# A graph layer pair on one core: VectorE scales the fourth of each four gathered chunks, GpSimd the other three

## The reference, cut to what matters

```python
    ex = jnp.exp(alpha - amax[dst])                             # one weight per edge and head
    denom = jax.ops.segment_sum(ex, dst, num_segments=n)
    attn = ex / jnp.maximum(denom[dst], 1e-10)
    out = jax.ops.segment_sum(h_src * attn[..., None], dst, num_segments=n)
    return out.reshape(n, H * D) + bias
x = _layernorm(x + _L1_gnn_ref(...), axis=-1)
```

## Time and profile before

| | |
|---|---|
| median of 3 runs | 3034.06 us (3033.27 to 3036.22) |
| the profiled execution, its own time | 3035.49 us |
| its span in the profile | 3033.7 us |
| granted TensorE clock, mean | 0.923 |
| busy over the span | PE 80%, DVE 56%, ACT 33%, POOL 62% |
| the weighted sum: from the first scale to the last add | 2730.5 to 2982.2 us |
| busy in 2780.77 to 2970.34 us (189.57 us, 320 adds, so 20 loop bodies) | PE 152.80, DVE 111.99, ACT 165.05, POOL 151.29 us |

### The profile page before, as it was taken

The page is one execution under the profiler, slowest core; times in us unless marked ns, Lnnn a source line. Parts: engine busy times, 40 slices in busy tenths (PEclk is TensorE's granted clock), DMA queues, the critical chain, the costliest instruction groups (busy, mean ns, idle before and its releaser), DMA issues.

```text
span 3033.7 us, 46185 instructions
## 1 busy us (share of the span) xinstructions
PE 2438.7 (80%) x9398; PEld 1579.2 (52%) x9399; DVE 1702.3 (56%) x4008; ACT 993.5 (33%) x2944; POOL 1880.7 (62%) x1739
## 2 busy tenths in 40 slices
PE   6999976477777679999899999999777767708882
PEld 5888843255555544445444454445555555506661
DVE  7765559899999940001344301113677666675557
ACT  1222221377777720000000000000433333318882
POOL 4777777787777870000067777760777777737774
PEclk9999999699999999999999999998888888859996
DMA  4000010355555555443344444452677777737772
GB/s 128 3 4 3 3 25 3 115 184 183 183 183 182 183 184 154 134 132 110 100 125 122 118 128 129 136 145 72 187 217 219 219 218 218 207 65 218 228 228 83
DMA packets 425353, 415.42 MB, mean 137 GB/s; under 512 B 85090, under 2 KB 411193, under 8 KB 424633
## 3 DMA queue, kind: packets, MB, share of 16 engines
q1 hardware_dynamic: 367385, 348.28, 36.8%
q0 software_dynamic: 57888, 66.23, 9.7%
HBM read 247.08 MB, written 167.17 MB: 137 GB/s over the span
## 4 chain that ended last, share of the span: by engine, by line
PE 54%; POOL 12%; issue 11%; DVE 7%; DVEq 4%; DMA 4%; ACT 3%; SPq 3%; ACTq 1%; POOLq 0%
PE psum L896 27%; POOL gath L618 7%; PE psum L826 5%; PE psum L708 5%; POOL rows_by_pair L579 5%; PE psum L693 3%; DVEq L400 2%; ACT lw L1084 2%; PE psum L888 2%; PE psum L968 2%; DMA gath<-gat_rows,rec 2%; SPq L484 2%; PE psum L1013 1%; PE psum L767 1%; PE psum L684 1%
## 5 line engine op out<-in xcount | busy, mean ns | idle before, releaser
L604 POOL DMA_INDIRECT rows_by_dst<-rec,place x392 | 381.6, 974 | 512.8 <-DVE place L1441 385.1
L896 PE MATMUL psum<-a_t,acc 128*128 128x512 f32 (+1 forms) x1400 | 553.7, 551 | 0.0
L589 POOL DMA_INDIRECT rows_by_low_digit<-rec,place x392 | 459.8, 1173 | 128.0 <-issue 128.0
L618 POOL DMA_INDIRECT gath<-gat_rows,rec x416 | 401.4, 965 | 214.1 <-issue 115.5
L826 PE MATMUL psum<-rhot,lw 128*128 128x256 f32 x1440 | 371.1, 414 | 169.7 <-ACT lw L1084 143.0
L579 POOL DMA_INDIRECT rows_by_pair<-rec,place x392 | 385.3, 983 | 161.9 <-issue 126.8
L826 PEld LDWEIGHTS psum<-rhot,lw 128*128 128x128 f32 x1440 | 281.9, 205 | 258.9 <-ACT lw L1084 182.2
L896 PEld LDWEIGHTS psum<-a_t,acc 128*128 128x128 f32 x1400 | 257.3, 195 | 272.1 <-issue 268.3
L1549 DVE SCALAR_TENSOR_TENSOR merged<-merged,same_of,psum 128x256 f32<-128x256 f32 x720 | 298.2, 476 | 19.1 <-PE psum L826 17.0
L896 PE MATMUL psum<-a_t,x 128*128 128x512 f32 (+1 forms) x700 | 294.4, 549 | 0.0
L1084 ACT ACTIVATE lw<-lhot,recs_pair 128x128 f32<-128x128 bf16 x720 | 228.5, 388 | 178.2 <-DVE lhot L1532 138.2
(11 more groups left out here) (311 smaller groups left out, 3301.9 us busy)
## 6 DMA issues: line engine op xcount, KB each, us to landing
a_t<-adjacency SPq DMA_DIRECT2D x450, 256.0 KB, 2.7
adjacency<-merged SPq DMA_DIRECT2D x721, 128.0 KB
gat_h_by_edge<-gath SPq DMA_DIRECT2D x104, 528.0 KB, 4.1
gath<-gat_h_by_edge SPq DMA_DIRECT2D x104, 528.0 KB, 4.1
gath<-gat_rows,rec POOLq DMA_INDIRECT x416
rows_by_pair<-rec,place POOLq DMA_INDIRECT x392
rows_by_low_digit<-rec,place POOLq DMA_INDIRECT x392
rows_by_dst<-rec,place POOLq DMA_INDIRECT x392
```

Source lines behind the costliest of these rows:

```text
L589: pool.indirect_dma_start(out=rows_low, in_=rec[:, c, :], out_offset=bass.IndirectOffsetOnAxis(ap=place[:, 1, c:c + 1], axis=0), in_offset ...
L604: pool.indirect_dma_start(out=rows_dst, in_=rec[:, c, :], out_offset=bass.IndirectOffsetOnAxis(ap=place[:, 0, c:c + 1], axis=0), in_offset ...
L618: pool.indirect_dma_start(out=gath[:, g % 4, c % 4, :], out_offset=None, in_=hh_dram, in_offset=bass.IndirectOffsetOnAxis(ap=rec_i[:, c, 0 ...
L896: i = pe.matmul(sums[b], table_g[:, w, b * P:(b + 1) * P], a_t[:, q % NA, 0:width(g)], start=False, stop=w == USED - 1)
```

## The change

VectorE gets a new instruction, `scale_fourth`: it scales the fourth chunk of a group, 128x256 elements, with both operands in SBUF. GpSimd's instruction is cut from four chunks to three. TensorE waits for the new semaphore `s_val4` before the fourth matmul of a group, and SyncE waits for it too before it refills a slot. The fourth chunks of groups 0 and 1 are scaled ahead of VectorE's wait for `s_clr`; the one of group g + 1 stands ahead of the adds of group g - 1, at even q ahead of the register load too. Four semaphores of earlier stages are folded into two others; each instruction still waits for the same event.

```diff
@@ -543,4 +543,5 @@
             for g in range(4, NQ):
                 sp.wait_ge(s_val, g - 3)
+                sp.wait_ge(s_val4, g - 3)
                 load_kept(g)
...
                     nc.gpsimd.tensor_tensor(
-                        val[:, q % 2, :, 0:D].rearrange("p c (h d) -> p c h d", h=HEADS),
-                        gath[:, q, :, 0:HX].rearrange("p c (h d) -> p c h d", d=HW)[:, :, :, 0:HD],
-                        s_sb[:, bass.ds(4 * g, 4), :].unsqueeze(3).broadcast_to([P, 4, HEADS, HD]),
+                        val[:, q % 2, 0:3, 0:D].rearrange("p c (h d) -> p c h d", h=HEADS),
+                        gath[:, q, 0:3, 0:HX].rearrange("p c (h d) -> p c h d", d=HW)[:, :, :, 0:HD],
+                        s_sb[:, bass.ds(4 * g, 3), :].unsqueeze(3).broadcast_to([P, 3, HEADS, HD]),
                         ALU.mult).then_inc(s_val, 1)
...
                     for j in range(4):
+                        if j == 3:
+                            pe.wait_ge(s_val4, g + 1)
                         if not (first and q < 2):
                             pe.wait_ge(s_add, 4 * (g - 2) + j + 1)
...
+            def scale_fourth(g, q, b, first):
+                dve.wait_ge(s_ld[q], 16 * (b + 1))
+                if not first:
+                    dve.wait_ge(s_mm, 4 * (g - 1))
+                v.tensor_tensor(val[:, q % 2, 3, 0:D].rearrange("p (h d) -> p h d", h=HEADS),
+                                gath[:, q, 3, 0:HX].rearrange("p (h d) -> p h d", d=HW)[:, :, 0:HD],
+                                s_sb[:, bass.ds(4 * g + 3, 1), :].rearrange("p c h -> p (c h)").unsqueeze(2)
+                                .broadcast_to([P, HEADS, HD]), ALU.mult).then_inc(s_val4, 1)
+
+            dve.wait_ge(s_exs, len(quads))
+            scale_fourth(0, 0, 0, True)
+            scale_fourth(1, 1, 0, True)
             dve.wait_ge(s_clr, 2)
 
             def sum_chunks(b, first, last):
                 for q in range(4):
                     g = 4 * b + q
+                    if not (first and q == 0) and not (last and q == 3):
+                        scale_fourth(g + 1, (q + 1) % 4, b + (q == 3), False)
                     if q % 2 == 0:
                         c = 1 + 4 * (g - 1)
...
-            act.wait_ge(s_seed, 1)
+            act.wait_ge(s_hist, 4)
...
-            dve.wait_ge(s_sum, 1)
+            dve.wait_ge(s_hist, 2)
...
-            dve.wait_ge(s_cum, 1)
+            dve.wait_ge(s_hist, 3)
...
-                dve.wait_ge(s_win, 1)
+                dve.wait_ge(s_ex, 2)
```

More of the change, by code:

```diff
@@ L271, in build @@
         s_oh = sem("onehots_built")
-        s_hist = sem("histogram_done")
+        s_hist = sem("histogram_product_done")
         s_part = sem("histogram_blocks_copied")
-        s_sum = sem("histogram_blocks_summed")
         s_hd = sem("histogram_step")
-        s_cum = sem("row_starts_summed")
-        s_seed = sem("table_seeded")
         s_hiT = sem("window_onehot_transposed")
@@ L302, in build @@
         s_place = sem("digit_places_ready")
-        s_ex = sem("window_starts_turned")
+        s_ex = sem("window_starts_turned_and_counted")
         s_exc = sem("window_starts_stored")
-        s_win = sem("windows_counted")
         s_low = sem("records_scattered_by_low_digit")
@@ L385, in build @@
         s_vx = sem("exp_columns_copied")
+        s_val4 = sem("fourth_chunk_scaled")
         s_mm = sem("chunk_summed")
@@ L671, in _ @@
             pe.wait_ge(s_part, 4)
-            pe.matmul(bank[1][0:HI, 0:LO], fold[:, :], blocks[:, :], start=True, stop=True).then_inc(s_sum, 1)
+            pe.matmul(bank[1][0:HI, 0:LO], fold[:, :], blocks[:, :], start=True, stop=True).then_inc(s_hist, 1)
             pe.wait_ge(s_hd, 6)
-            pe.matmul(bank[1][0:HI, 0:1], triu[0:HI, 0:HI], small[:, 0:1], start=True, stop=True).then_inc(s_cum, 1)
+            pe.matmul(bank[1][0:HI, 0:1], triu[0:HI, 0:HI], small[:, 0:1], start=True, stop=True).then_inc(s_hist, 1)
             pe.wait_ge(s_hd, 10)
             pe.matmul(bank[2][0:HI, 0:LO], identf[0:HI, 0:HI], table0[:, :], start=True, stop=False,
-                      skip_group_check=True).then_inc(s_seed, 1)
+                      skip_group_check=True).then_inc(s_hist, 1)
             def spread(t, s, n, cold):
@@ L757, in dst_windows @@
                 pe.wait_ge(s_exc, 2)
-                pe.matmul(bank[7][0:1, 0:NC], ones[0:USED, 0:1], started[0:USED, :], start=True, stop=True).then_inc(s_win, 1)
+                pe.matmul(bank[7][0:1, 0:NC], ones[0:USED, 0:1], started[0:USED, :], start=True, stop=True).then_inc(s_ex, 1)
                 yield
```

## The result

| | before | changed |
|---|---|---|
| median | 3035.14 us (3033.27 to 3036.54, 4 runs) | 3069.1 us (3067.64 to 3071.76, 4 runs) |
| ratio, 95% interval | | 1.0112 (1.0100 to 1.0124): slower |
| the profiled execution, its own time | 3035.49 us | 3068.21 us |
| its span | 3033.7 us | 3066.0 us |
| start of the first scale | 2730.52 us | 2731.55 us |

The forecast was 3066 us in a range of 3050 to 3088. The median is 34.0 us longer and the span of the profiled execution 32.3 us. Of that 31.2 us lie in the stage, 1.0 us ahead of it and nothing behind it. Of the change only the folded semaphores reach ahead of the stage.

A forecast was written before the change was run, and what follows sets the result against it. VectorE's own stream of adds and register loads was taken as the bound: 17.0 us at odd q, 12.3 at even q and 2.8 at the start make 32.1 us, so a median of 3066 us, range 3050 to 3088.

The forecast's parts named there:

- What bounds the stage: Stage 2730 to 2982 us: VectorE's adds and register loads are the bound, not GpSimd; four groups take 9.49 us.
- Odd q: Multiply between two groups' adds costs one datapath step, 0.34 us, 50 times: 17.0 us.
- second rival: VectorE's multiply slips into the adds' latency and costs nothing; only the start is left, 3037 us; chance 5%.
- Even q: Multiply ahead of the register load costs only sequencer steps, 0.18 us, or 0.31 at the loop's head: 12.3 us.
- The wait of the even multiply for the products: Ahead of the register load: products known at T + 2.65, margin 0.1 to 0.2 us, cost 0; otherwise 10 us.
- T: Time of VectorE's first add behind a register load (2853.88 us in the profile before).
- The collision: GpSimd's multiply holds VectorE's even multiply until T + 4.2; it ends at T + 4.5, hidden by the register load.
- third rival: The register load waits for a held multiply: 1.4 us in each of 50 pairs, 70 us more, 3136 us; chance 9%.
- GpSimd's time: GpSimd's instruction loses some 478 of 1913 ns, 104 times; it becomes idle time, value 0.
- The start: At the stage's start the first add of group 1 comes 2.8 us later, behind products and register load.
- The clock's case: Fourth rival: longer TensorE pauses lower its clock in the stage ten times, 15 us more, 3081 us; chance 14%.

The follow-up runs named there:

- e1: Kernel before, GpSimd scaling only three of four chunks, the fourth left as ones, nothing added to VectorE: ratio 0.9994, stage 251.0 us.
- e11: Kernel before with four slots of scaled rows in `val` instead of two: 3036.0 us against 3036.0, ratio 1.0000, stage 251.5 us.
- e3: Changed kernel with GpSimd's multiply cut to 8 columns of one chunk a group: ratio 1.0073 against the kernel before, stage 282.6 us.
- e7: Kernel before with four window numbers per register load instead of eight, each used twice: ratio 0.9962, stage 235.9 us.
- e5: Changed kernel with VectorE's multiply only between two groups' adds, GpSimd scaling four chunks of the other groups: ratio 1.0044, stage 270.0 us.
- e4: Changed kernel with VectorE's multiply only ahead of the register load, GpSimd scaling four chunks of the other groups: ratio 1.0045, stage 271.1 us.
- e2: Changed kernel with the even multiply moved behind the register load: ratio 1.0175 against the kernel before, stage 326.2 us.
- e9: Kernel before with window numbers packed in pairs (four loaded, taken apart in the sequencer), plus the change: ratio 0.9996, stage 253.9 us.
- e0: Changed kernel again, no edit, on other chips: 4293.0 us against 4260.1 for the kernel before, ratio 1.0084, stage 283.9 us.
- e6: Kernel before with the four folded semaphores alone: 4261.8 us against 4257.0, ratio 1.0010, stage 251.2 us.

## Why the prediction was right, point by point

- **What bounds the stage.** VectorE's own stream, and in it the register load, was the bound. e1 and e11 loosen GpSimd and change nothing, and so does e3 for the changed kernel; e7 shortens the load and gains the 16 us that it was expected to gain. This was the step on which everything hung, and it was read from the order in time against the name in the list of waits.
- **Odd q.** Forecast 0.34 us, measured 0.333, e5 alone 0.34. 50 x 0.333 = 16.7 us (17.0). The second rival, a free multiply, falls.
- **Even q.** Forecast 0.18 and 0.31 us, measured 0.23 and 0.32 us: 25 x 0.23 + 25 x 0.32 = 13.7 us (12.3).
- **The wait of the even multiply for the products.** At q = 2 of the body shown, ScalarE learns of the products at 2868.58, T + 2.65 as forecast, and VectorE's multiply begins at 2868.98, 3.05 behind its first add. The margin holds in the change. In e4, without the odd multiply ahead, it doesn't, and costs about 0.12 us each time: the condition that the prediction named.
- **The collision.** GpSimd's instruction was forecast at T + 2.8 and came at T + 2.79; its end, T + 4.2 forecast, was T + 4.27; the multiply's end T + 4.5 forecast, T + 4.55 measured; the second GpSimd instruction meets no multiply. The third rival (the load waits for the held multiply) falls by the chain above: the load starts 1.1 us ahead of the multiply's end. e3 shows that the hold costs nothing here, e2 what it costs without its cover, and e9 that half the load with its register operations still just covers it.
- **GpSimd's time.** A quarter off 1913 ns is 1435 ns; measured 1482. 256 of 1024 elements took 431 ns with them, not 478, so some 190 ns of the instruction don't depend on its size.
- **The start.** Forecast 2.8 us; 1.3 us in the first pair of profiles (from the first scale to the first add of group 1: 9.33 and 10.67 us), 2.8 us in e0 (12.15 us). The forecast took the products of group 1 to be known as late as before, 9.8 us behind the first scale. In the first profile they came at 8.7 us, by ScalarE's timeline of the changed kernel:

```profile
2740.29 0.20 ACT L1227 COPY ht<-digits 128x32 f32<-128x32 f32 x1
```

and VectorE's:

```profile
2740.34 1.55 DVE L1795 TENSOR_TENSOR ht<-gath,digits 128x256 f32<-128x256 f32 x1
...
2742.22 0.43 DVE L1789 TENSOR_TENSOR acc<-acc,psum 128x264 f32 x1 [0.33 <-PE psum L1013]
```

From the multiply's start to the add it is 1.88 us, near the 2.2 that were taken. In e0 the products came at 10.0 us. The difference between the two goes with the clock: 0.74 in 2735 to 2740 us of the changed kernel (row below) where the kernel before has 0.58, and 0.50 in e0. At like clocks the change costs the start 1.8 us (the changed kernel against e6) and 2.8 us (e0 against the kernel before). So the path of the forecast was right, and the low clock of the kernel before was tacitly carried over; in the first profile it didn't come so. No term of the forecast says which clock an execution gets there. That the start goes with it is shown by four executions side by side; no run sets the clock.
- **The clock's case.** In the steady stage TensorE's pauses grew to 1.31 and 1.74 us, near the forecast's 1.4 to 1.8, and the clock stayed full from 2740 to 3014 us. By stretch of the changed kernel (length; busy time and count of PE, PEld, DVE, ACT, POOL; clock; DMA share; GB/s):

```profile
2735.00:2740.00 5.00, 4.98 (x16) 3.69 (x16) 1.45 (x5) 4.73 (x15) 1.65 (x1) 0.74 0.65 211
2835.00:2885.00 50.00, 36.49 (x155) 28.28 (x154) 42.21 (x96) 38.05 (x112) 27.06 (x19) 1.00 0.68 204
```

and the first stretch of the kernel before:

```profile
2735.00:2740.00 5.00, 5.00 (x14) 3.87 (x14) 1.88 (x5) 4.08 (x12) 1.91 (x1) 0.58 0.52 162
```

The prediction leaned on the pauses staying shorter than the 2.26 us of its row. The same stage of the kernel before shows that the length of one pause doesn't decide it:

```profile
707.19 5.38 PE L826 MATMUL psum<-rhot,lw 128*128 128x256 f32 x16 [1.99 <-ACT lw L1084]
...
730.51 3.89 PE L826 MATMUL psum<-rhot,lw 128*128 128x256 f32 x16 [2.27 <-ACT lw L1084]
```

Behind 1.99 us the clock was low (0.72 in 707 to 713 us) and behind 2.27 us it wasn't (1.00 in 730 to 736 us). So the clock's case was nearer than the prediction had it; that it didn't come with pauses of 1.74 us is what the run shows, and no run tests how far off it was.

The sum of the measured terms is 16.7 + 13.7 + 1.3 = 31.7 us; the stage is 31.2 us longer. That the forecast of 32.1 us is within 1 us of it is in part luck: the even multiplies came out 1.4 us larger than forecast, and the start 1.5 us smaller in this profile. In e0, with the start at its 2.8 us, the stage is 32.3 us longer. The span's 32.3 us contain 1.0 us from ahead of the stage, within the scatter there.

## What to carry to other kernels

Before work is moved between engines, find in the timeline which engine's own stream is closed in time: an engine that waits can give its work away for nothing, but nothing is gained either. A "wait for TensorE" in front of VectorE may be VectorE's own sequencer loading registers; compare the time at which the named engine was done, and shorten the load first. Work that must be added to such a stream costs only a few sequencer steps ahead of the load, and a full datapath step between two instructions that otherwise run back to back. Its cover is only as long as the load and the register operations behind it.

## What the runs showed of the hardware

- A load of 8 registers from SBUF keeps VectorE's sequencer for 1.85 us and one of 4 for 0.97 us, about 0.22 us a register. VectorE's datapath goes on meanwhile with what it was given before. The kernel before issues 51 of the long ones in this stage, some 94 us of 252.
- A VectorE multiply with both operands in SBUF that starts while GpSimd's runs is held until GpSimd's ends and is done 0.28 us later (up to 1.5 us instead of 0.42 in the steady stage). The sequencer doesn't wait for it: the load began 0.15 us behind its start.
- The hold goes the other way too: where VectorE's multiply began 0.04 us ahead of GpSimd's (3959.49 and 3959.53 us in e0), GpSimd's took 1.73 us instead of 1.48.
- The granted clock stayed at 1.00 (2.4 GHz) with TensorE pausing 1.31 and 1.74 us in turn, once in each pair of groups. In the earlier stage it was low behind pauses of 1.99 and 2.26 us and full behind one of 2.27 us.
